# An attention block on one core: x kept on chip, row broadcast by TensorE, maxima one slot later, two batches projected in the set-up step

## The reference

```python
def _sln(h, w, ...):                       # layer norm, modulated by the condition w
    ln = (h - mean) / sqrt(var + EPS) * ln_g + ln_b
    gamma, beta = (w @ Wg.T + bg)[:, None, :], (w @ Wb.T + bb)[:, None, :]
    return gamma * ln + beta

h = _sln(x, cond, ...)
q, k, v = split(h @ Wqkv.T + bqkv)         # 16 heads of 16 columns
att = softmax(einsum('bhqd,bhkd->bhqk', q, k), axis=-1) / D ** 0.5
out = einsum('bhqk,bhkd->bhqd', att, v) @ Wp.T + bp
h1 = out + x
return _sln(h1, cond, ...) + h1            # one output: 16 x 256 x 256
```

## Time and profile before

| | |
|---|---|
| median of 3 runs | 408.3 us (407.98 to 411.03) |
| the profiled execution's own time | 412.25 us |
| its span | 410.4 us |
| mean granted TensorE clock | 0.967 of 2.4 GHz |
| PE, PEld busy | 359.5 us (88%), 300.6 us (73%) |
| DVE, ACT, POOL busy | 298.1 us (73%), 235.5 us (57%), 121.6 us (30%) |
| chain that ended last | PE 49%, DMA 22%, SP's queue 18%, DVE 5% |
| DMA | 50334 packets, 53.68 MB, mean 131 GB/s; first of 40 slices 206 GB/s |

### The profile page before, as it was taken

How to read it: one execution, slowest core, us unless ns; L and a number is a source line. 1 busy time by engine, 2 the same in 40 slices (tenths; PEclk the granted TensorE clock), 3 DMA queues, 4 the chain that set the end, 5 groups by cost and what they waited for, 6 DMA issues and landing times.

```text
span 410.4 us, 8984 instructions
## 1 busy us (share of the span) xinstructions
PE 359.5 (88%) x3208; PEld 300.6 (73%) x3209; DVE 298.1 (73%) x730; ACT 235.5 (57%) x437; POOL 121.6 (30%) x108
## 2 busy tenths in 40 slices
PE   3856579798989999998999899999899999988972
PEld 3636478687878788887878687878787888857652
DVE  7714738476878788786878787887787886977454
ACT  8320227466666767575657566665667575755750
POOL 5310403142415142332424242424142323030332
PEclk9986969899999999999999999999999999999996
DMA  6179895969598799969897969899979989590221
GB/s 206 37 96 127 116 106 103 162 100 161 115 174 114 157 158 128 186 108 181 119 192 109 180 112 180 126 175 121 174 123 124 168 108 181 101 184 10 81 78 51
DMA packets 50334, 53.68 MB, mean 131 GB/s; under 512 B 6610, under 2 KB 41825, under 8 KB 50290
## 3 DMA queue, kind: packets, MB, share of 16 engines
q1 hardware_dynamic: 50290, 53.11, 78.7%
HBM read 14.18 MB, written 4.23 MB: 45 GB/s over the span
## 4 chain that ended last, share of the span: by engine, by line
PE 49%; DMA 22%; SPq 18%; DVE 5%; issue 4%; ACT 1%; POOL 1%; POOLq 0%; DVEq 0%
DMA kst<-qk_l 19%; PE m L689 16%; SPq L288 15%; PE st L689 11%; PE sa L689 9%; PE pv L689 9%; DMA qst<-m_l 2%; SPq L291 2%; PE pv L784 2%; DVE mx L489 1%; DVE qst L640 1%; PE pv L837 1%; PE pv L798 1%; SPq L301 1%; DVE y L600 0%
## 5 line engine op out<-in xcount | busy, mean ns | idle before, releaser
L489 DVE TENSOR_REDUCE mx<-sa 128x2 f32<-128x512 f32 x256 | 174.3, 683 | 90.6 <-PE sa L689 86.3
L467 ACT ACTIVATE p<-st 128x512 f32<-128x512 f32 x256 | 150.5, 597 | 101.8 <-PE st L689 99.6
L689 PE MATMUL sa<-kst,qst 128*128 128x256 f32 x512 | 107.8, 294 | 31.9 <-DMA kst<-qk_l 31.1
L689 PE MATMUL st<-qst,kst 128*128 128x256 f32 x512 | 112.8, 303 | 1.4 <-ACT p L467 0.7
L689 PEld LDWEIGHTS sa<-kst,qst 128*128 128x128 f32 x512 | 80.5, 194 | 37.8 <-DMA kst<-qk_l 28.0
L689 PEld LDWEIGHTS st<-qst,kst 128*128 128x128 f32 x512 | 79.6, 193 | 23.2 <-ACT p L467 15.2
L689 PE MATMUL pv<-p,v_st 128*32 128x256 f32 x1024 | 68.5, 385 | 0.3 <-ACT p L467 0.3
L357 POOL TENSOR_TENSOR hT_l<-hT,hT_h 128x512 fp32r<-128x512 f32 x16 | 20.6, 1285 | 100.3 <-ACT hT_h L400 100.3
L371 POOL TENSOR_TENSOR rstd<-vare,minus_half 128x4 f32<-128x4 f32 (+1 forms) x21 | 18.8, 893 | 95.5 <-DVE vare L544 92.0
L376 POOL TENSOR_TENSOR h1b<-h,gb 128x512 f32<-128x512 f32 x16 | 20.6, 1285 | 87.2 <-DVE h L573 87.2
L689 PEld LDWEIGHTS pv<-p,v_st 128*32 128x32 f32 x1024 | 26.7, 109 | 20.2 <-ACT p L467 0.5
(11 more groups left out here) (95 smaller groups left out, 537.2 us busy)
## 6 DMA issues: line engine op xcount, KB each, us to landing
qst<-qk_h SPq DMA_DIRECT2D x64, 128.0 KB
qst<-qk_l SPq DMA_DIRECT2D x64, 128.0 KB
kst<-qk_h SPq DMA_DIRECT2D x64, 128.0 KB
kst<-qk_l SPq DMA_DIRECT2D x64, 128.0 KB
xa<-x_dram SPq DMA_DIRECT2D x16, 256.0 KB, 4.0
xd<-x_dram SPq DMA_DIRECT2D x16, 256.0 KB, 3.4
gb<-gb_rows SPq DMA_DIRECT2D x16, 256.0 KB, 3.7
out_dram<-y SPq DMA_DIRECT2D x16, 256.0 KB, 4.0
```

The source lines that it names most:

```text
L467: nc.scalar.activation(p32[:, h % PR, :], st_ps[h % 2][:], ACT.Exp).then_inc(exp_done, 1)
L489: dve.tensor_reduce(mx[:, par(a), h // HH, (h % HH) * TT:(h % HH + 1) * TT], sa_ps[h % 2][:].rearrange("p (t n) -> p t n", t=TT), AX.X, AL ...
L689: return nc.tensor.matmul(o, l, r, start=start, stop=stop)
```

## The change

- `LEAD` goes: `scores_max(b + 1, h)` and `maximum(b + 1, h)` stand in slot h.
- `qst` and `kst` have 67 rows instead of 128: 64 rows of parts, a zero row in `qst` (against ones in `kst`), and the two maxima rows. The first pass contracts over 65 rows (without the maxima rows), the second over 67. The fixed rows are written once, by four transfers; the zero-row copy of each group goes, and so does the zeroing of the whole tiles.
- x is loaded once into one of `NX = 6` buffers `xbuf(a)`. `add_bias` adds the bias into it in place and the residual reads it; `xd` goes. The load of batch b + 4 now also waits for h1 of batch b - 2.
- The rows of gamma and beta are no longer written to DRAM. They stay in SBUF as a high part (16 partitions) and a low part (16 more) in `gb_hl`. In slot 3 of step b PE multiplies them with `pick_b`, a 0/1 column for batch b - 2 repeated over 128 columns, made by POOL in slot 2; ACT evicts the result into `gb` in slot 4.
- POOL does `h1b` in slot 6 instead of 1 and `norm_x` in slot 7 instead of 5.
- The first step (-2) projects q and k of batch 0 in its slots as before, and behind slot 11 those of batch 1; the transposes of the rows, bias_b and wp_l (`set_up_rows` on PE and DVE) move behind batch 0's q and k. `warm_up` has 8 matmuls and stands ahead of step -2. PE and ACT run one step more at the end, for gb.

The core of the diff:

```diff
-ROWS = 4 * HD + 2
+ZERO_ROW = 4 * HD
+ROWS = ZERO_ROW + 3
 VC = 2 * HD
 LAG = 3
-LEAD = 1
 PR = 8
 
 Q_SLOTS, K_SLOTS, V_SLOTS, P_SLOTS = (0, 1, 3, 4), (1, 3, 4, 5), (7, 7, 8, 9), (11, 12, 13, 15)
-S_MT1, S_AT, S_MT0, S_XT = 1, 8, 10, 11
+S_MT1, S_GB, S_AT, S_MT0, S_XT = 1, 3, 8, 10, 11
 S_QH, S_KH, S_VH = 5, 6, 10
-WARM = 14
-NSTK = 9
+WARM = 8
+NSTK = 8
+NX = 6
...
             sp.wait_ge(consts_ready, 4)
-            sp.wait_ge(pad_k_zero, 1)
-            sp.wait_ge(pad_1_zero, 2)
-            sp.dma_start(raw(kst[4 * HD:ROWS]).rearrange("r p h n -> r (p h n)"), ones[:]).then_inc(ones_in, 16)
-
-            sp.wait_ge(gbrow_ready, 1)
-            sp.dma_start(gb_dram, gbrow[:]).then_inc(gb_out, 16)
-
-            sp.wait_ge(gb_out, 16)
+            for r in range(ZERO_ROW, ROWS):
+                sp.dma_start(raw(kst[r:r + 1]).rearrange("a p h n -> a (p h) n"),
+                             ones[0:2 * H, :]).then_inc(fixed_rows_in, 16)
+            sp.dma_start(raw(qst[ZERO_ROW:ZERO_ROW + 1]).rearrange("a p h n -> a (p h) n"),
+                         zrows[:]).then_inc(fixed_rows_in, 16)
...
                                  raw(src)).then_inc(s, 16)
-                if t == 0:
-                    sp.dma_start(raw(qst[4 * HD:ROWS, p, g * HH:(g + 1) * HH, :]), zrows[:]).then_inc(s, 16)
...
+                    wait(sp, h1_ready, 1 * (b - 2) + 1)
+                    sp.dma_start(xbuf(b + 4), x_t[b + 4]).then_inc(x_in[par(b + 4)], 16)
                 stack(b + 2, 0, 0)
                 stack(b + 2, 0, 1)
                 maxima(b + 1, 0)
-                if has(b):
-                    wait(sp, y_ready, 1 * (b - 2) + 1)
-                    sp.dma_start(xd[:, par(b)], x_t[b]).then_inc(xd_in[par(b)], 16)
-                    sp.dma_start(gb[:, par(b)], gb_dram[b].rearrange("(a n) -> a n", a=1)
-                                 .broadcast_to([P, 2 * D])).then_inc(xd_in[par(b)], 16)
+                if first(b + 1):
+                    sp.wait_ge(gbl_ready, 1)
+                    sp.wait_ge(gb_zero, 1)
+                    sp.dma_start(raw(gb_hl[B:2 * B, :]), raw(gb_l[:])).then_inc(gbl_in, 16)
...
-                wait(pool, xd_in[par(a)], 32 * (half(a) + 1))
-                pool.tensor_tensor(xd[:, par(a)], xd[:, par(a)],
+                wait(pool, xn_ready, 1 * a + 1)
+                pool.tensor_tensor(xbuf(a), xbuf(a),
...
-                    if h == 1 and has(b - 2):
+                    if h == 2 and has(b - 2):
+                        wait(pool, gb_done, 1 * (b - 3) + 1)
+                        pool.tensor_copy(pick_b[:], pick[:, b - 2:b - 1].broadcast_to([P, P])).then_inc(pick_b_ready, 1)
+                    if h == 6 and has(b - 2):
+                        wait(pool, gb_ready, 1 * (b - 2) + 1)
                         wait(pool, h1_ready, 1 * (b - 2) + 1)
                         wait(pool, y_ready, 1 * (b - 3) + 1)
                         pool.tensor_tensor(h1b[:], h1[:],
-                                           gb[:, par(b - 2), D:2 * D].rearrange("p (a n) -> p a n", a=1)
+                                           gb[:, D:2 * D].rearrange("p (a n) -> p a n", a=1)
                                            .broadcast_to([P, TT, D]), ALU.add).then_inc(h1b_ready, 1)
-                    if h == 5 and has(b + 3) and not first(b + 3):
+                    if h == 7 and has(b + 3) and not first(b + 3):
...
+                    if h == S_GB + 1 and has(b - 2):
+                        wait(act, gb_done, 1 * (b - 2) + 1)
+                        wait(act, y_ready, 1 * (b - 3) + 1)
+                        nc.scalar.activation(gb[:], pv_ps[0][:], ACT.Copy).then_inc(gb_ready, 1)
+                    if h == S_QH and not first(b + 1):
+                        high_q(b + 2)
+                    if h == S_KH and not first(b + 1):
+                        high_k(b + 2)
...
+                    if h == 15 and first(b + 2):
+                        high_q(1)
+                        high_k(1)
...
-            act.wait_ge(consts_ready, 1)
-            for pad in (kst, qst):
-                nc.scalar.activation(pad[:, 1].rearrange("p h n -> p (h n)"),
-                                     ones[:, 0:1].broadcast_to([P, H * N]), ACT.Copy, scale=0.0).then_inc(pad_1_zero, 1)
...
                     wait(dve, h1b_ready, 1 * a)
                     dve.tensor_tensor(h1[:].rearrange("p t n -> p (t n)"), m1[:],
-                                      xd[:, par(a)].rearrange("p t n -> p (t n)"), ALU.add).then_inc(h1_ready, 1)
+                                      xbuf(a).rearrange("p t n -> p (t n)"), ALU.add).then_inc(h1_ready, 1)
...
+            def set_up_rows():
+
+                dve.wait_ge(vecs_ready, 1)
+                for k in range(KT):
+                    o = dve.tensor_scalar(bias_cols[:, k, :], ones[:, 0:P], vecs[:, 6, k:k + 1], D ** -0.5, ALU.mult, ALU.mult)
+                o.then_inc(bias_cols_ready, 1)
+                dve.wait_ge(gbrow_done, 1)
+                dve.wait_ge(gb_zero, 1)
+                dve.tensor_copy(gb_hl[0:B, :], st_ps[0][0:B, :]).then_inc(gbh_ready, 1)
+                dve.wait_ge(gbh_ready, 1)
+                dve.tensor_tensor(gb_l[:], st_ps[0][0:B, :], gb_hl[0:B, :], ALU.subtract).then_inc(gbl_ready, 1)
+                dve.wait_ge(wph_ready, 1)
+                dve.tensor_tensor(wp_l[:], wp[:], wp_h[:], ALU.subtract).then_inc(wpl_ready, 1)
+
+                dve.wait_ge(bias_done, 1)
+                dve.tensor_copy(bias_b[:], st_ps[1][:, 0:D]).then_inc(bias_ready, 1)
...
+                if first(b + 2):
+                    between[(12, 1)] = [set_up_rows]
+                    between[(15, 0)] = [lambda: low_qk(1, 0, m0, qh_ready, ql_ready)]
+                    between[(15, 1)] = [lambda: low_qk(1, 1, m1, kh_ready, kl_ready)]
+                if first(b + 1):
+                    del between[(5, 1)], between[(6, 1)]
                 for h in range(H):
                     for part in between.get((h, 0), []):
                         part()
-                    i = h + LEAD
-                    maximum(b + 1 + i // H, i % H)
+                    maximum(b + 1, h)
...
-            dve.memset(raw(qst[:, 0]), 0.0).then_inc(pad_v_zero, 1)
...
-                    o = mm(sa_ps[h % 2][:, t * N:(t + 1) * N], qst[:, p, h, t * P:(t + 1) * P],
-                           kst[:, p, h, :], True, True)
+                    o = mm(sa_ps[h % 2][:, t * N:(t + 1) * N], qst[0:ZERO_ROW + 1, p, h, t * P:(t + 1) * P],
+                           kst[0:ZERO_ROW + 1, p, h, :], True, True)
...
+                    wait(pe, gb_ready, 1 * (b - 2) + 1)
...
+            def set_up_rows():
+
+                pe.wait_ge(gfull_ready, 1)
+                for i, w in enumerate((gfull, bfull)):
+                    for k in range(KT):
+                        o = nc.tensor.transpose(st_ps[0][0:B, (2 * i + k) * P:(2 * i + k + 1) * P], w[:, k, :],
+                                                ident[:])
+                o.then_inc(gbrow_done, 1)
+
+                pe.wait_ge(wp_in, 16)
+                pe.wait_ge(bias_cols_ready, 1)
+                for k in range(KT):
+                    mm(st_ps[1][:, 0:D], bias_cols[:, k, :], wp[:, k, :], k == 0, False)
+                mm(st_ps[1][:, 0:D], ones[0:1, 0:P], row[:, 2 * D:3 * D], False, True).then_inc(bias_done, 1)
...
-                    if h == H - LEAD and first(b + 2):
-                        pe.wait_ge(zeros_ready, 1)
-                        warm_up(WARM)
                     if has(b):
                         scores(b, h)
-                    i = h + LEAD
-                    scores_max(b + 1 + i // H, i % H)
+                    scores_max(b + 1, h)
...
+                    if h == S_GB and has(b - 2):
+                        if first(b - 2):
+                            pe.wait_ge(gbl_in, 16)
+                        wait(pe, pick_b_ready, 1 * (b - 2) + 1)
+                        wait(pe, ml_ready, 2 * min(b, B - 1) + 2)
+                        wait(pe, att_ready, 2 * min(b - 1, B - 1) + 1)
+                        mm(pv_ps[0][:], pick_b[:], gb_hl[:], True, True).then_inc(gb_done, 1)
...
+                    if h == S_XT and first(b + 2):
+                        set_up_rows()
+                        wait(pe, hTl_ready, 2)
+                        wait(pe, kl_ready, 1)
+                        for quarter in range(4):
+                            project_qk(1, 0, m0, q_done, quarter)
+                        for quarter in range(4):
+                            project_qk(1, 1, m1, k_done, quarter)
...
+            pe.wait_ge(zeros_ready, 1)
+            warm_up(WARM)
```

127 lines of the change are left out of this document (57 added, 70 removed).

## The result

The change gains nothing: median 412.85 us (20 runs) beside 409.47 us (20 runs) of the kernel before, ratio 1.0056 with a 95% interval of 1.0029 to 1.0083, so the kernel after is 0.3 to 0.8% slower here, and no different in its second timing (e5). The ratio leaves out executions more than about 1.5% over the fastest of their kernel, and the profiled one of the kernel after, 1.9% over, is such a one; stretches of half clock as in its step 14 stand in faster executions too (e3, e6, and e1 in the kernel before). The prediction was 397.4 us, range 390.5 to 404.0. (The rest of the miss, 1.5 us, is mostly that the kernel before had 408.3 us in the first three runs.)

A forecast was written before the change was run, and what follows sets the result against it. It took PE's 12.1 us of waiting for row-copy DMAs in twelve steps as the bound, PE itself close behind. Gains 8.6 + 3.8 + 0.2 - 0.4 - 1.3 = 10.9 us, from 408.3 to 397.4 us, range 390.5 to 404.

The forecast's parts named there:

- Start: Set-up and steps 0 and 1: batch 2 starts at 91.4 instead of 99.98, 8.6 us gained (bounds 6 and 11).
- Steps 2 to 13: Steady steps: 21.6 us each for steps 2 to 12, 21.1 for step 13, a gain of 3.8 us.
- (a): Steady steps, maxima one slot later: the row buffer is needed only after the new step's first scores, not in slot 15.
- (b): Steady steps, fewer transfers: a group of row copies lands 10.4 us after its first issue instead of 11.24.
- the DMA loop of 21.25 us: Steady steps, first scores to next through copies and maxima row: 9.9 + 0.25 + 10.4 + 0.4 + 0.3; PE at 21.6 hides it.
- (c): Steady steps, gb by PE: one more matmul of 512 columns on the path, 0.24 us a step.
- (d): Steady steps, h1b moved on POOL: add_bias collides with VectorE's y, PE waits for aT_l, 0.5 us a step (at most 0.9).
- The prediction's own sign: Steady steps: if PE waits over 0.5 us a step for `m_l` or `kst`, the fewer-transfers term is wrong.
- End: Step 15 loses 0.4 us to the eviction and matmul; h1b after rstd in the last batch loses 1.3.
- No collision: Rival, steady steps: y reaches the port first or POOL is further on; 5.5 us more gained, 391.9 us; chance 0.20.
- The copies land no sooner: Rival: groups still take 11.1 us, slot 0 waits for maxima, the steps gain nothing; 403.2 us; chance 0.20.
- Slower: Rival: `m_l` lands by its own time, not behind the group; steps of 23.25 us, 418.4 us in all; chance 0.05.

The follow-up runs named there:

- e5: The kernel after, unchanged, timed and profiled again: 413.02 us, ratio 1.0028 to the kernel before.
- e3: The kernel after, with add_bias on GpSimd waiting for the first half of y on VectorE: 409.23 us, ratio 0.9963 to the kernel before.
- e6: The kernel after, with the low part of the q and k bias written by VectorE to partition 32, without a DMA: 412.97 us, ratio 1.0052.
- e1: The kernel before, with only its score matmuls narrowed from 128 to 66 rows: 419.25 us, ratio 1.0202.
- e4: e2 with blocks of 300 gapless matmuls behind its work, over 126, 97, 65 and 33 rows; only the clock and matmul times are read.
- e2: The kernel after, with scores over 126 and 128 rows, the added rows zeroed once at the start: 413.29 us, ratio 1.0047 to the kernel before.
- e7: e2 with the zeroing moved, parity 1 to GpSimd behind hT_l of batch 1, its fixed rows after the first copies: 412.63 us, ratio 1.0070.
- e9: The kernel before, with only the maxima scores and the maxima moved one head slot later (LEAD 0): 408.86 us, ratio 0.9953.
- e10: e7 with the fixed rows of parity 1 issued after the third group of copies: 410.18 us, ratio 0.9994 to the kernel before.
- e12: e11 with the scores over 126 and 128 rows as in e10: 405.81 us, ratio 0.9866 to the kernel before.
- e14: e12 with the maxima's DMAs issued by ScalarE as in e13: 416.13 us, ratio 1.0122 to the kernel before.
- e15: e10 with blocks behind its work of 3 to 5 matmuls a round, paced by ScalarE, over 126 or 65 rows; only the clock is read.
- e8: The kernel after, with matmuls of zeros in TensorE's two waits of the start: 409.48 us, ratio 0.9984 to the kernel before.
- e11: The kernel after with the edits of e3, e6 and e8, and h1b before rstd in the last step: 407.82 us, ratio 0.9879.
- e13: The kernel after, with the maxima's DMAs issued by ScalarE on a queue of their own: 424.23 us, ratio 1.0343 to the kernel before.
- e16: The kernel after, with the first maxima of batch 0 issued ahead of the third group of copies: 419.18 us, 412.48 for the kernel before.

## Why the prediction was wrong, point by point

**The step that is missing: the rows of the score matmuls.** The diff narrows them from 128 to 65 and 67 rows. The prediction counted what their zeroing had cost ("The big memsets go") and nothing else of it; it had a matmul cost what its columns cost. That is so at a given clock (0.120 us at 65, 97 and 126 rows in e4). But the rows also weigh on the clock where PE has little else to do: in the first steps, and at the head of step 14, which has no q and k projections. Half clock in the nine wide and nine narrow kernels profiled (before, e2, e4, e7, e9, e10, e12, e14, e15; after, e1, e3, e5, e6, e8, e11, e13, e16), means:

| us at half clock in | steps 0 and 1 | steps 2 to 13 | step 14 | length of step 14 |
|---|---|---|---|---|
| wide | 6.5 | 0 (none in any) | 1.1 (0 to 3.4) | 20.07 |
| narrow | 11.0 | 3.8 (0 to 13.65) | 6.8 (0 to 13.65) | 21.58 |

In steps 2 to 14 that is 9.5 us more at half clock; work that fills PE takes half of them less at full, so 4.7 us. That is an estimate from the mean over scattered executions of kernels that differ in more than their rows, and it is an upper one: with 3.4 us of half clock step 14 took 19.5 to 20.0 us in three narrow kernels (e3, e6, e16) and 21.3 to 21.4 in three wide ones (e2, e7, e10), so its length doesn't go by the clock alone. Only e1 times the rows alone: 2.0% in the kernel before. In the kernel after their share stays open: e10 is 0.6% under it, e2 and e7, whose starts suffer from the zeroing, are not, and between e11 and e12 nothing can be told. The forecast of 0.2 us gained in step 14 failed mainly by this: 4.2 us were lost there, and e1 loses 3.7 us by the rows alone (22.98 for 19.25).

**Start: 8.6 forecast, 1.7 found,** the largest part of the miss. The chain of the kernel after, set-up and first steps:

```profile
8.54 7.14 DMA rows<-row_l
...
15.77 4.27 PE m L721 x21
...
21.42 0.63 SPq L291
...
25.96 7.75 DMA kst<-qk_l
...
46.97 4.83 DMA qst<-m_l
...
51.94 0.77 PE st L721 x2
```

q started at 15.77, not 14.5, because the one-row DMA of its bias now ended last. In the kernel before it landed 1.8 us after its issue at 10.55, ahead of hT_l; here it was issued 2 us earlier, while loads still filled the DMA engines (share 0.99 from 8 to 9 us), and took 7.14 us; why so long, when the share was 0.22 to 0.34 from 10 to 13 us, is open. The prediction had no term for it. And q's matmuls took 4.27 us, inside the bounds but not the 3.3 I took, half clock having come back in that wait. Together 1.9 us on the first copies (21.42 for 19.5); e6, without that DMA, has them at 19.08. From the first copies to the first scores it then took 30.5 us, where 28.6 were forecast (18.7 for two groups, 9.2 for x and the third, 0.7 for the maxima). That the maxima stand behind the third group was foreseen, and e16 shows it right: with that undone the first scores are at 47.67. Steps 0 and 1 took 46.4 us instead of 43.3; 11.6 us of half clock lie in them. e8 fills the waits and has 6.8 us there and 44.2 us. So 3.8 us of the miss are the copies' start and length, and of the 3.1 in steps 0 and 1 the clock has at least the 2.2 that e8 took back. The rows have some part in it (e1 had 10.7 us of half clock there, the kernel before 7.9).

**Steps 2 to 13: 3.8 forecast, 2.1 found.** (a) Right: the wait for the copies is gone. (b) Mis-sized: the DMA loop of 21.25 us, which PE "just hides", and in it the 0.8 us by which fewer transfers were to let a group land earlier. The chain of one step of the kernel after, from its first scores to the next:

```profile
184.67 0.50 PE st L721 x2
...
202.05 0.55 SPq L302
202.64 3.62 DMA qst<-m_l
206.26 0.04 issue
206.30 0.50 PE st L721 x2
```

SyncE's first issue of the group was at 195.03, 10.36 us into the step (forecast 10.15), the maxima had landed 11.23 us later (forecast 10.8): the loop is 21.63 us, not 21.25. e9, which keeps all the transfers, has 11.17 us in its step; by the landings of the `m_l` transfers the mean over steps 2 to 12 is 11.4 us in e9 and 11.3 in the kernel after, so dropping the transfers brought 0.1 to 0.2 us and not 0.8. That the maxima land behind the copies was right: in e3 they are issued 0.6 us earlier after the group's first issue (7.04 us for 7.61) and land 11.08 us after it. e3, e9 and e12 have steps of 21.66, 21.59 and 21.56, with PE waiting 6.6 to 8.4 us for these transfers in twelve steps. Taking PE's load away gives nothing there. The prediction's own sign, PE waiting over 0.5 us a step for `m_l`, was not met in the kernel after (0.34) and is in e3 (0.59). The move of the maxima alone is worth 3.4 us in twelve steps (e9); the rest of the change, x on chip against one more matmul a step, minus 1.3. (c) Right: PE is 0.25 us a step busier. (d) Right in mechanism, wrong on the path. y's first half beside add_bias:

```profile
197.07 1.44 DVE L614 SCALAR_TENSOR_TENSOR y<-h,mv,gb 128x256 f32<-128x256 f32 x2
```

for 0.87, 0.57 us more (0.7 forecast; add_bias ended at 197.83, so a full block would have been 0.76), and PE waited 1.8 us for aT_l in twelve steps, 0.15 a step and not 0.5 (the prediction's own figures, 180.3 for 179.92, give 0.4). With the loop at 21.6 it was worth nothing (e3). That a step of 21.70 us was found where 21.6 was forecast is luck: the forecast has it from this collision, the runs from the DMA loop.

**End: -1.7 forecast, -2.6 found.** h1b came after rstd as forecast and cost its 1.3 us (the last y began 1.37 us after rstd ended, 0.09 in the kernel before); the collision, which was already there, cost more: y took 1.52 and lay ahead of aT_l in the chain, for which PE waited 2.1 us instead of 1.4. Step 15 itself needed 0.3 us more up to its last oT (15.4 us after the scores of head 0, for 15.1), 0.4 forecast.

**The rivals.** *No collision* is refuted by e3: without it the steps stay. *The copies land no sooner* was right in the direction: the last copies landed some 10.8 us after the first issue, between its 11.1 and the forecast's 10.4, and slot 0 waits for the maxima rows behind them. But the steps gained over half of the forecast where it had them gain nothing. *Slower* by a maxima row that lands by its own time did not happen, 3.62 us after its issue is soon enough; e13 made maxima land late, by order. (Its 418.4 subtracts the 5.1 us of the rival above it; with its own start it would be 416.4.) What the profile was to show: scores of batch 0 near 48.1, the y mean above 570 ns and the vanished wait for `kst<-qk_l` were good marks; the first failed (51.94, past the 50 that was to say the start is wrong), the other two came true without bringing the time.

## What to carry to other kernels

Read a diff for the shape of each matmul as well as for its count: rows that hold zeros cost no time in the matmul, and taking them away can cost the clock wherever PE has only such matmuls beside another engine's work; zeroing them once has its own price at the start. Before pricing a wait at its length, work out the next loop to the same accuracy; here it was 0.4 us a step longer than worked out, and it set the steps. A small transfer on the path landed early here only where little stood before it in the DMA engines (e16 against e13); its place in the order of issues counted, not the queue.

## What the runs showed of the hardware

- The granted clock went by the rows of the contraction as well as by how busy PE was: full at 126 rows and 1.2 GHz at 65 in otherwise equal streams, with PE shown busy 32.88 of 33 and 40.00 of 40 us (e15); in a gapless stream it stayed full at 126, 97 and 65 rows and fell at 33 (e4). The Trainium skill ("TensorE: Matmul & The Clock Gate", "Part 1: The HAM clock gate") lets the clock go by how busy the engine has been and does not speak of rows; the measurement goes further.
- Two transfers of 8 KB, alone on their queue, landed 11.4 and 11.1 us after their issue while another queue moved groups of copies of 1 MB (e13), and within 2.6 us of the first issue where the engines were idle at their issue (e16). By the Trainium skill ("DMA: Bandwidth & Descriptors", "Queues, rings and completion order") an engine takes turns between the queues that have work, packet by packet, which would have brought them through early; this trace does not agree, and why is open.
- A GpSimd memset of 3.5 us held up a VectorE cast (3.50 for 0.42 us) and a tensor_scalar (e2), but in e7 two such memsets left subtractions of VectorE that read PSUM at 0.69 us.
